# Decay exponents inside a scan tile from differences of bf16 parts, and another order of the last context tile

## The reference, cut to what matters

```python
zxbcdt = _rms(x, norm_w) @ in_proj_w
z, xBC = ...                                    # 512 and 768 columns
dt = jax.nn.softplus(zxbcdt[..., -H_M:] + dt_bias)          # 8 heads
xBC = jax.nn.silu(conv(xBC))                    # 4 taps along the rows
xh, Bm, Cm = ...                                # 8 heads x 64, 128, 128
A = -jnp.exp(A_log); decay = jnp.exp(dt * A); dbx = dt[..., None] * xh
def step(h, inp):
    dec, u, bt, ct = inp
    h = h * dec[:, :, None, None] + u[..., None] * bt[:, None, None, :]
    y = jnp.einsum('bhpn,bn->bhp', h, ct)
    return (h, y)
h0 = jnp.zeros((b, H_M, HEADDIM, D_STATE), x.dtype)
y = ys + D_skip[None, None, :, None] * xh
u = _rms(y * jax.nn.silu(z), gnorm_w)
return resid + u @ out_proj_w
```

## Time and profile before

| what | before |
|---|---|
| median of 3 runs (lowest to highest) | 1530.23 us (1529.27 to 1531.14) |
| the profiled execution | 1529.02 us |
| its span | 1527.4 us |
| mean granted clock of TensorE | 0.965 |
| busy TensorE, weight loads, DVE, ACT, POOL | 1355.9, 1007.1, 1053.9, 1065.7, 97.1 us |
| context stage | to about 176 us |
| scan stage | about 176 to 350 us |
| attention stage | from about 350 us |

### The profile page before, as it was taken

The page is one execution under the profiler, slowest core; times in us unless marked ns, Lnnn a source line. Parts: engine busy times, 40 slices in busy tenths (PEclk is TensorE's granted clock), DMA queues, the critical chain, the costliest instruction groups (busy, mean ns, idle before and its releaser), DMA issues.

```text
span 1527.4 us, 35942 instructions
## 1 busy us (share of the span) xinstructions
PE 1355.9 (89%) x13426; PEld 1007.1 (66%) x13426; DVE 1053.9 (69%) x2343; ACT 1065.7 (70%) x3209; POOL 97.1 (6%) x151
## 2 busy tenths in 40 slices
PE   7899899998998889999888999988889999788855
PEld 6788566666666556777666667766666777566644
DVE  4766667766788778677777767877776787777400
ACT  4566567756778887777887677787876777887422
POOL 2100122220000000000000000000000000000000
PEclk9999999999999999999999999999999999999855
DMA  8232310003131112122011112200121121010100
GB/s 294 74 97 97 115 44 1 1 1 125 47 96 41 56 57 84 38 68 64 29 57 57 57 57 57 84 29 29 57 84 42 43 84 57 29 38 20 42 1 14
DMA packets 69883, 90.42 MB, mean 59 GB/s; under 512 B 5520, under 2 KB 58896, under 8 KB 69328
## 3 DMA queue, kind: packets, MB, share of 16 engines
q1 hardware_dynamic: 69600, 87.87, 18.2%
q0 software_dynamic: 112, 0.26, 0.1%
...
## 4 chain that ended last, share of the span: by engine, by line
PE 62%; DVE 13%; ACT 13%; issue 10%; POOL 0%; DMA 0%; ACTq 0%; DVEq 0%; SPq 0%; POOLq 0%
PE ps L1251 13%; PE ps L1593 11%; PE ps L1258 8%; PE ps L1265 7%; PE ps L1622 6%; ACT arena L755 5%; DVE arena L1200 5%; PE ps L1667 3%; PE ps L1328 2%; PE ps L1420 2%; PE ps L1437 2%; PE ps L1576 2%; ACT R L815 1%; PE ps L1393 1%; DVE arena L914 1%
## 5 line engine op out<-in xcount | busy, mean ns | idle before, releaser
L1251 PE MATMUL ps<-W,arena 128*128 128x128 f32 x2896 | 429.4, 282 | 22.3 <-ACT arena L755 19.8
L755 ACT ACTIVATE arena<-ps,nmax 128x512 f32<-128x512 f32 x640 | 435.1, 686 | 0.4 <-issue 0.2
L1251 PEld LDWEIGHTS ps<-W,arena 128*128 128x128 f32 x2896 | 320.8, 144 | 170.4 <-issue 128.4
L762 ACT COPY arena<-ps 128x512 f32<-128x512 f32 x320 | 187.2, 585 | 209.7 <-PE ps L1251 205.6
L1180 DVE TENSOR_REDUCE nmax<-ps 128x1 f32<-128x512 f32 x320 | 206.1, 686 | 118.8 <-PE ps L1593 80.9
L1200 DVE COPY arena<-ps 128x512 f32<-128x512 f32 x320 | 213.7, 686 | 24.9 <-PE ps L1251 14.5
L1593 PE MATMUL ps<-W,arena 32*128 32x512 f32 x1280 | 184.4, 643 | 36.5 <-DVE arena L1200 35.1
L1622 PE MATMUL ps<-arena 128*32 128x128 f32 x5120 | 173.8, 277 | 31.8 <-ACT arena L762 31.6
L1183 DVE TENSOR_REDUCE nmax<-ps 128x2 f32<-128x1024 f32 x160 | 193.7, 1211 | 0.0
L1622 PEld LDWEIGHTS ps<-arena 128*32 128x32 f32 x5120 | 130.7, 110 | 69.7 <-ACT arena L762 59.2
L755 ACT ACTIVATION_READ_ACCUMULATOR arena<-ps,nmax 128x1 f32 x640 | 131.1, 205 | 0.0
...
## 6 DMA issues: line engine op xcount, KB each, us to landing
...
```

Of the source, the lines that this page charges most:

```text
L755: nc.scalar.activation(Pr[:, a, :], ps[:, a, :], ACT.Exp, bias=nmax[:, u % 32:u % 32 + 1], accum_out=den[:, u % 32:u % 32 + 1]).then_inc(s ...
L762: nc.scalar.copy(PT[:, (4 * Q + a) % 8, :, :].rearrange("p k n -> p (k n)"), psT).then_inc(sem("u_ev_act"), 1)
L1251: ins = nc.tensor.transpose(dst[:, k * P:(k + 1) * P], src[:, k * P:(k + 1) * P], ident)
```

## The change

The exponents inside a tile are computed in another way. The running sum S of dt*A over the rows of a tile comes from one product with the triangle for all tiles (`decay_sums`). DVE splits S into three bf16 parts (`decay_parts`); TensorE turns them, 16 pieces (`decay_turns`), so that rows are in the columns: `cs_j` holds the parts of S_j and ones, `cs_i` those of S_i and minus ones, signs arranged so that one product over 48 rows gives S_i - S_j. GpSimd spreads `cs_j` over 8 heads with the 0/1 pattern `head8` (`head_rows`), two tiles in one instruction. For each tile TensorE now puts a bf16 triangle `shut`, 0 where j <= i and -1e30 elsewhere, into X[1] and X[2] through a bf16 identity (two products, L1484 of the new kernel), and adds the differences (two products over half the rows, L1490). The Exp of -1e30 is 0, so DVE no longer multiplies C.B with a triangle. In the tiles of c = 0 the state is zero, and its read, its decay and its add are left out; the states are no longer zeroed, and DVE copies the first increment. The three products for the decays and their Exp (`decays`) come inside tile 0, and there the Exp of the exponents comes behind the copies. In the context stage the softplus and ACT's Exp come one tile earlier (k = 14), and in the last tile (k = 15) both `items` come before `ctx_keys` and `ctx_values`.

```diff
...
+Z_AT = [2 * k - min(k, NB) for k in range(NT + 1)]
+Y_AT = [4 * k - 2 * min(k, NB) for k in range(NT + 1)]
...
-        dAm = sb("dAm", [P, HM, P])
+        dAm = sb("dAm", [P, 2, HM, P], BF16)
...
+                if k == NT - 3:
+                    pool.wait_ge(sem("c_tpn"), NT)
+                    pool.memset(cs_parts[:, :, :, :], 0.0).then_inc(sem("zeroed"), 1)
+                    pool.wait_ge(sem("zeroed"), 3)
+                    pool.memset(cs_parts[:, 0, :, 32:56], 1.0)
+                    pool.memset(cs_parts[:, 1, :, 0:24], -1.0).then_inc(sem("zeroed"), 1)
...
+            def head_rows(m):
+                nc.gpsimd.tensor_tensor(dAm[:, m % 2, :, :], cs_j[:, m, :].unsqueeze(1).to_broadcast([P, HM, P]),
+                                        wide(w("head8"), P), ALU.mult).then_inc(sem("m_dAm"), 1)
...
+                if k % 2 and k + 3 < NT:
                     pool.wait_ge(sem("m_rows"), 2 * k + 1)
-                    masked_dA(k + 1)
+                    head_rows((k + 3) // 2)
...
+                if k == NT - 2:
+                    act.wait_ge(sem("m_steps"), 3)
+                    nc.scalar.activation(dts[:, 3, :, :], dts[:, 2, :, :], ACT.Exp).then_inc(sem("m_steps_act"), 1)
+                    nc.scalar.activation(negA[:, :], w("alog"), ACT.Exp).then_inc(sem("m_steps_act"), 1)
                 if k:
                     silu(k - 1, 0)
+                if k == NT - 1:
+                    keep_item(k, 0)
+                    keep_item(k, 1)
+                if k == NT - 1:
+                    act.wait_ge(sem("m_steps"), 23)
+                    nc.scalar.copy(cs_parts[:, 1, :, 32:56], cs_parts[:, 0, :, 0:24]).then_inc(sem("m_steps_act"), 1)
                 ctx_keys(k)
+                if k == NT - 1:
+                    act.wait_ge(sem("m_cs"), 4)
+                    nc.scalar.copy(cs_i[:, :, :], cs_T[0][:, :, :]).then_inc(sem("m_steps_act"), 1)
                 if k % NCH == 0:
                     keep_xT(k // NCH)
-                keep_item(k, 0)
+                if k < NT - 1:
+                    keep_item(k, 0)
                 if k:
                     silu(k - 1, 1)
                 ctx_values(k)
-                if k == NT - 2:
-                    act.wait_ge(sem("m_soft"), 3)
-                    nc.scalar.activation(dts[:, 3, :, :], dts[:, 2, :, :], ACT.Exp).then_inc(sem("m_exp"), 1)
-                    nc.scalar.activation(negA[:, :], w("alog"), ACT.Exp).then_inc(sem("m_exp"), 1)
-
-            keep_item(NT - 1, 1)
+
...
+            nc.scalar.activation(warm[:, :], col("bk3", 0), ACT.Exp)
...
+            def decays():
+                act.wait_ge(sem("m_cs"), 5)
+                nc.scalar.activation(dec[:, :, :, :].rearrange("p g k n -> p (g k n)"), item[0][:, 0:3 * NT * HM],
+                                     ACT.Exp).then_inc(sem("m_dec"), 1)
...
+                    if k == 0:
+                        intra_weights()
+                        decays()
...
+            def decay_parts():
+                cs = side[0][0][:, 0:NT * HM].rearrange("p (k h) -> p k h", k=NT)
+                part = lambda i: cs_parts[:, 0, :, HM * i:HM * i + HM]
+                nc.vector.tensor_copy(ident_b, ident)
+                nc.vector.tensor_scalar(shut, w("tri_le"), 1.0, 1e30, ALU.subtract, ALU.mult)
+                dve.wait_ge(sem("m_cs"), 1)
+                dve.wait_ge(sem("zeroed"), 4)
+                nc.vector.tensor_copy(part(0), cs).then_inc(sem("m_steps"), 1)
+                dve.wait_ge(sem("m_steps"), 20)
+                nc.vector.tensor_tensor(d(9), cs, part(0), ALU.subtract).then_inc(sem("m_steps"), 1)
+                dve.wait_ge(sem("m_steps"), 21)
+                nc.vector.tensor_copy(part(1), d(9)).then_inc(sem("m_steps"), 1)
+                dve.wait_ge(sem("m_steps"), 22)
+                nc.vector.tensor_tensor(part(2), d(9), part(1), ALU.subtract).then_inc(sem("m_steps"), 1)
+
+            def decay_rows():
+                dve.wait_ge(sem("m_cs"), 2)
+                nc.vector.tensor_copy(cs_j[:, 0, :], cs_T[2][:, 0, :]).then_inc(sem("m_steps"), 1)
+                dve.wait_ge(sem("m_cs"), 3)
+                nc.vector.tensor_copy(cs_j[:, 1:, :], cs_T[1][:, 1:, :]).then_inc(sem("m_steps"), 1)
...
+                if k == NT - 2:
+                    softplus_front()
+                if k < NT - 1:
+                    ctx_keys(k)
...
-                    softplus_front()
+                    softplus_series()
+                    softplus()
                 if k == NT - 1:
-                    softplus()
+                    decay_parts()
+                    ctx_keys(k)
+                    decay_rows()
                 conv(k, 0)
+                if k == NT - 1:
+                    conv(k, 1)
...
-                    nc.vector.tensor_tensor(r.BG[:, 1, :], X[0][:, P:2 * P], w("tri_le"), ALU.mult).then_inc(sem("m_M"), 1)
-                    dve.wait_ge(sem("m_M"), 2 * k + 1)
-                    nc.vector.tensor_tensor(r.seg, r.seg, r.BG[:, 1, :].unsqueeze(1).to_broadcast([P, HM, P]),
+                    dve.wait_ge(sem("m_E"), k + 1)
+                    nc.vector.tensor_tensor(r.seg, r.seg, X[0][:, P:2 * P].unsqueeze(1).to_broadcast([P, HM, P]),
...
+                    if c == 0:
+                        dve.wait_ge(sem("m_state"), k + 1)
+                        nc.vector.tensor_copy(Hst[:, b, :], X[3]).then_inc(sem("m_H"), 1)
+                    elif k < FT:
...
+            def decay_sums():
+                pe.wait_ge(sem("c_act"), NT - 1)
+                pe.wait_ge(sem("m_steps"), 19)
+                mm(side[0][0][:, 0:NT * HM], w("tri_le"), dts[:, 11, :, :].rearrange("p a h -> p (a h)"), start=True,
+                   stop=True).then_inc(sem("m_cs"), 1)
+
+            def decay_turns():
+                pe.wait_ge(sem("m_steps_act"), 4)
+                pe.wait_ge(sem("c_dve"), NT - 1)
+                for v in (1, 0):
+                    for m in range(NT // 2):
+                        ins = nc.tensor.transpose(cs_T[2 if v and m == 0 else v][:, m, :],
+                                                  cs_parts[:, v, 2 * m:2 * m + 2, :].rearrange("p k n -> p (k n)"), ident_b)
+                        if v and m == 0:
+                            ins.then_inc(sem("m_cs"), 1)
+                    ins.then_inc(sem("m_cs"), 1)
+
             ctx_turn(0)
             for k in range(NT):
                 if k + 1 < NT:
                     ctx_turn(k + 1)
+                if k == NT - 1:
+                    items(k, 0)
+                    items(k, 1)
+                if k == NT - 1:
+                    decay_sums()
                 ctx_keys(k)
-                items(k, 0)
+                if k == NT - 1:
+                    decay_turns()
+                if k < NT - 1:
+                    items(k, 0)
                 ctx_values(k)
-                items(k, 1)
+                if k < NT - 1:
+                    items(k, 1)
...
+                    m, rows = k // 2, slice(k % 2 * 64, k % 2 * 64 + 64)
+                    if k == 0:
+                        pe.wait_ge(sem("m_steps"), 25)
                     for i in range(2):
-                        ins = mm(X[1 + i], w("tri_gt"), dAm[:, 4 * i:4 * i + 4, :].rearrange("p h n -> p (h n)"),
-                                 start=True, stop=True)
+                        mm(X[1 + i].rearrange("p (h n) -> p h n", n=P), ident_b, shut.unsqueeze(1).to_broadcast([P, 4, P]),
+                           start=True, stop=False)
+                    pe.wait_ge(sem("m_dAm"), k // 2 + 1)
+                    if k == 0:
+                        pe.wait_ge(sem("m_steps_act"), 5)
+                    for i in range(2):
+                        ins = mm(X[1 + i], cs_i[rows, m, :], dAm[rows, m % 2, 4 * i:4 * i + 4, :].rearrange("p h n -> p (h n)"),
+                                 start=False, stop=True)
                     ins.then_inc(sem("m_rows"), 1)
...
+                    if k == 0:
+                        pe.wait_ge(sem("m_fa"), NB * XG - 1)
+                        for q, name in enumerate(("tri_le", "tri_gt", "ones")):
+                            ins = mm(item[0][:, q * NT * HM:(q + 1) * NT * HM], w(name), dts[:, 11, :, :].rearrange("p a h -> p (a h)"),
+                                     start=True, stop=True)
+                        ins.then_inc(sem("m_cs"), 1)
...
-                    pe.wait_ge(sem("m_E"), k + 1)
                     if c:
+                        pe.wait_ge(sem("m_E"), k + 1)
                         pe.wait_ge(sem("m_H"), k - NB + 1)
-                    mm(X[1], xs[:, 5, part], Hst[:, b, :], start=True, stop=True).then_inc(sem("m_z"), 1)
+                        mm(X[1], xs[:, 5, part], Hst[:, b, :], start=True, stop=True).then_inc(sem("m_z"), 1)
...
+        "head8": ((i[:, None] % 8 == np.arange(8)) & (i[:, None] % 32 < 24)).astype(np.float32),
```

137 lines of the change are left out of this document (66 added, 71 removed).

## The result

| | before | after |
|---|---|---|
| median of 5 runs each, on the same chip | 1529.80 us | 1515.57 us (1514.23 to 1521.4) |
| ratio, 95% interval | | 0.9915 [0.9897, 0.9933] |
| profiled execution, span | 1529.02, 1527.4 us | 1517.49, 1515.9 us |
| mean granted clock | 0.965 | 0.961 |
| z product (L1420, L1521 of the new kernel) of tile 0, tile 1 | 190.36, 201.47 | 183.65, 193.94 |

What follows compares the result with a forecast made beforehand. TensorE bounds tiles 1 to 12, with ACT's square-then-Exp order 0.38 us behind; hand-over 6.0, tiles 2 and 3 1.2, tiles 4 to 12 3.3: 10.5 us off, 1519.5 us. Own range 1516.5 to 1522; 8 in 10: 1515 to 1526.5.

Steps and rivals of the forecast that it cites:

- The Exp then starts when ACT's square ends: Scan tiles: with row sums faster, the next Exp waits for ACT's square and starts 0.38 us sooner.
- The rival of all 0.86 us coming through: Scan tiles: ACT's order does not bind, the full row-sum saving counts; 16 us off, 1514 us; chance 0.05.
- the one of a cycle that doesn't gain: Scan tiles: Exp or square slips with DVE, GpSimd's product stretching L1033; only 6.0 us off, 1524.2 us; chance 0.10.
- Tiles 1 to 12: Scan stage: 1.2 us off in tiles 2 and 3, 3.3 us off in tiles 4 to 12.
- L1443 to the Exp's end 3.54: Cycle of tiles 2 and 3: first part 3.54 us (0.27, 2.18, 1.09), within a forecast cycle of 9.52 us.
- DVE without the triangle product: Scan tiles: L1031 gone, L1033 starts 0.3 us sooner, but DVE has idle time; gain 0.
- Hand-over: From context to scan tiles: tile 1's z product 4.4 to 6.9 us sooner, taken as 6.0 us.
- two convolutions 4.64: Hand-over on DVE: the last two convolutions take 4.64 us and end at 181.4 us.
- GpSimd: 0: GpSimd's masked product, one for two tiles, is no earlier on any path than before; gain 0.
- the early fall: Hand-over: 1.3 us of TensorE waiting at 173.7 plus 16 turns could drop the clock from 175 us.
- The rival of the longer low clock: Hand-over: clock falls at 175 or 184, stays low through tile 1; gain 10.5-4.2, time 1523.7 us; chance 0.19.
- Attention "unchanged to 0.5 us": Attention stage, over three quarters of the time: untouched by the change, moves as a block, unchanged to 0.5 us.

Runs made afterwards that it cites:

- r1: The kernel after with two more unused bf16 products of 512 columns ahead of every tile's row sums; 1517.53 us, ratio to before 0.9921.
- r2: The kernel after with four more unused bf16 products of 512 columns ahead of every tile's row sums; 1525.07 us, ratio to before 0.9964.
- v1: The kernel after with the square still on ACT, but behind the next tile's Exp and copies; 1510.09 us, ratio to before 0.9893.
- v2: The kernel after with the square moved from ACT to DVE, behind the state's add; 1508.16 us, ratio to before 0.9858.
- a0: The kernel after, run again unchanged; 1516.83 us, ratio to before 0.9907.
- mb: The kernel before with only GpSimd's memset of the states moved to the end of the context stage; 1526.48 us, ratio to before 0.9986.
- p1: The kernel after with GpSimd's second masked product held back until DVE's convolutions are done; 1515.77 us, ratio to before 0.9917.
- dz: The kernel after with an unused product shaped like the state read, waiting for the Exp, in tiles 0 to 3; 1519.55 us, ratio to before 0.9935.
- fill: The kernel after with 20 unused products keeping TensorE busy before tile 0's copies; 1514.61 us, ratio to before 0.9906.

## Why the prediction was right, and where its sizes were off

The median of 1515.57 us lies inside the range given for 8 in 10, 1515 to 1526.5, and 0.9 us below the forecast's own, 1516.5 to 1522. The mechanism forecast for the tiles is what happened. That the time came out so near is in part luck: terms that were wrong or left out went both ways, as the parts below show.

*The bound.* Right. "The Exp then starts when ACT's square ends" is what the timeline, r1, r2, v1 and v2 show, with one correction: it starts 0.1 us before the accumulator read ends. The weight load of the state read stands idle for 0.30 us until the Exp ends, in the tile shown; about 0.5 was forecast. The rival of all 0.86 us coming through is out (cycle 9.60, not 9.25), and so is the one of a cycle that doesn't gain.

*Tiles 1 to 12: 6.1 us, 4.5 forecast.* The term "L1443 to the Exp's end 3.54" was too long: it is 3.41 (256.19 to 259.60), since the Exp follows the square's start by 0.63 us (257.90 to 258.53), while I had let it wait for the accumulator read's end, 0.73 in the earlier trace rows. So 9.60 stands against 9.73 from tile 4 on. In tiles 2 and 3 this term is 3.34 and the step from the Exp's end to z 0.70 instead of 0.80, the rest 5.28 instead of 5.18: 9.31 against 9.52. On TensorE four bf16 products of the kernel cost 1.06 us (257.10 to 258.16), not 0.86, where r2's four in a row take 0.87. Inside a pair they are 0.22 us apart as forecast; from L1484 to L1490 and from there to L1496, where the product goes from 128 rows to 64 and back, it is 0.31 us. That the change of rows is the cause is likely, but no run tests it. The 0.2 us lie inside TensorE's slack.

*DVE without the triangle product.* Right: 0. L1094, one operand in PSUM, takes 1.22 us in every tile; L1033 took up to 1.95.

*Hand-over: 5.5 us, 6.0 forecast, by two errors that met.* (7.53 at tile 1's z, less 2.0 of memset and start.) Take the softplus's end as zero; the forecast has it at 167.3, the trace at 165.25. Then (forecast, measured): parts made 7.3, 6.5; turned rows in SBUF 9.4, 8.4; last convolution ended 14.1, 15.5; rows of tile 0 in SBUF 17.2, 18.35. DVE was 1 us ahead of my list when the two last convolutions began, since I took 1.8 us for the parts and they take 1.46, and it lost 2.57 there. The step that failed is "two convolutions 4.64": GpSimd's two products lie beside them, and the six steps take 7.21. I had named this cost for L1033 only, in a rival. The trace of before had it in view; these are its convolutions, the last two beside L466:

```profile
168.81 2.32 DVE L914 SCALAR_TENSOR_TENSOR arena<-arena,W 128x512 f32<-128x512 f32 x3
...
176.75 3.83 DVE L914 SCALAR_TENSOR_TENSOR arena<-arena,W 128x512 f32<-128x512 f32 x3
...
181.17 3.83 DVE L914 SCALAR_TENSOR_TENSOR arena<-arena,W 128x512 f32<-128x512 f32 x3
```

The kernel before thus lost 3.0 us there, more than the 2.57 of the kernel after: it is the forecast that left the cost out, and not the change that brought it in.

Behind it the forecast of tile 1's z was 194.6 to 197; it came at 193.94, with 2.0 us of start and memset in it, and at 193.24 in a0: the 0.5 us between 6.0 and 5.5 are no more than executions differ by.

*GpSimd: 0.* Wrong twice, by the same mechanism: 1.4 us gained where the memset went (mb), 2.57 lost against the forecast beside the convolutions (p1 shows 1.5 of it, for one of the two; the other 1.1, beside the product that p1 leaves in place, is read off the timeline only). I had read the queue of GpSimd only for what it starts late, not for what it does to DVE.

*The clock.* It fell where forecast (181 to 194) and not at 175: TensorE waited 0.68 us and turned for 1.07, and the clock of 176 to 180 is 1.00. The Trainium skill (TensorE: Matmul & The Clock Gate, Part 4: PE-mode transpose) says that a transpose in TensorE's transpose mode doesn't count as busy in the way a matmul does. By that rule the early fall was the likelier, and it did not come. But the wait was half of the 1.3 us forecast, and no run here had the longer one; nor does the trace show in which mode the turns ran. So the rule is not refuted. The rival of the longer low clock rested on a misreading: before, the clock was not down for 14 us on end. A window of before (columns as in the earlier trace rows) has it back at 1.00 in between; it was low from about 180 to 183.4 and from 186.9 to 193.7:

```profile
184.00:186.00 2.00, 0.00 (x0) 0.00 (x0) 1.00 (x1) 0.95 (x2) 0.45 (x1) 1.00 0.63 239
```

*Attention "unchanged to 0.5 us".* Wrong: 2.1 us more after, 4.0 more in a0, 1.0 less in r1, 1.6 less in v2, with the same instructions. In the two profiles it goes with stretches of low clock ahead of the last 86 us (which are low in all): 13.6 us in two stretches before, 27.3 in six after. But their sum isn't all of it: dz had the 13.6 us of before and took 1169.9, 2.4 less than before. What sets these falls stays open; that the change makes them more frequent isn't shown, as r1, which has the change too, had 17, and fill 10.2.

*The time.* 13.6 us at the start of attention, 10.5 forecast: 1.6 more in the tiles, 1.4 for the memset, 0.6 by the start, 0.5 less in the hand-over. Attention took 2.1 back, and the median lies 1.9 below the profiled execution, where I had set it 1.2 above.
